# Layer 0 of a two-layer attention/FFN kernel: the band mask moves from a TensorE matmul into VectorE's row maximum

## The reference

```python
q, k, v = split(x @ w_in.T + b_in)                 # 8 heads of 8 channels, t = 256
scores = einsum('bqhd,bkhd->bhqk', q, k) / sqrt(d)
band = abs(idx[:, None] - idx[None, :]) <= 64      # local attention
scores = where(band, scores, neg)
attn = softmax(scores, axis=-1)
o = einsum('bhqk,bkhd->bqhd', attn, v) @ w_out.T + b_out
out = einsum('nit,io->not', relu(o^T) * encodings, w_ct) + b_ct
```

## Time and profile before

| | |
|---|---|
| median of 3 runs | 1429.04 us (1427.28 to 1431.03) |
| span of the profiled execution | 1429.4 us |
| TensorE, VectorE, ScalarE, GpSimd busy | 92%, 67%, 61%, 50% of the span |
| layer 0's attention, loads and weight preparation before it included | up to about 584 us |
| layer 0's FFN and the change of layers | about 584 to 700 us |
| layer 1's attention and FFN | from about 700 us |

### The profile page before, as it was taken

How to read it: one execution, slowest core, us unless ns; L and a number is a source line. 1 busy time by engine, 2 the same in 40 slices (tenths; PEclk the granted TensorE clock), 3 DMA queues, 4 the chain that set the end, 5 groups by cost and what they waited for, 6 DMA issues and landing times.

```text
span 1429.4 us, 37785 instructions
## 1 busy us (share of the span) xinstructions
PE 1315.2 (92%) x11332; PEld 910.0 (64%) x11332; DVE 955.8 (67%) x2156; ACT 874.6 (61%) x1909; POOL 716.5 (50%) x1292
## 2 busy tenths in 40 slices
PE   1999999999999998882799999999999989999998
PEld 1666777777777776571466666666666655766675
DVE  6438878787888787468888888888888872111110
ACT  1147676666666667563488888888888875122211
POOL 6336777777777776404555655656656511010000
PEclk9869999999999999995799999999999999999999
DMA  8314444444344443001434444444444410000000
GB/s 243 78 36 95 103 100 90 96 100 100 90 96 100 100 90 87 6 12 37 92 91 104 105 95 103 103 97 104 102 97 107 93 41 1 15 30 15 15 15 29
DMA packets 90797, 111.18 MB, mean 78 GB/s; under 512 B 15056, under 2 KB 82384, under 8 KB 83056
## 3 DMA queue, kind: packets, MB, share of 16 engines
q1 hardware_dynamic: 83184, 103.38, 31.9%
q10 hardware_dynamic: 7552, 7.02, 1.7%
HBM read 16.52 MB, written 4.19 MB: 14 GB/s over the span
## 4 chain that ended last, share of the span: by engine, by line
PE 62%; POOL 11%; issue 11%; DVE 8%; ACT 2%; ACTq 1%; DMA 1%; POOLq 1%; SPq 1%; DVEq 1%
PE bank L459 10%; PE bank L420 8%; PE bank L652 8%; PE bank L643 8%; PE bank L436 7%; PE bank L418 5%; PE bank L470 4%; DVE row_max L1031 3%; PE bank L501 3%; POOL rot L1216 2%; PE bank L614 2%; POOL Qp L1205 2%; PE bank L490 1%; POOL k_rest L1221 1%; POOL q_rest L1201 1%
## 5 line engine op out<-in xcount | busy, mean ns | idle before, releaser
L1031 DVE TENSOR_REDUCE row_max<-bank 128x2 f32<-128x384 f32 (+1 forms) x1024 | 599.6, 617 | 148.5 <-PE bank L420 146.8
L687 ACT ACTIVATE probs<-bank 128x384 f32<-128x384 f32 (+1 forms) x1024 | 534.4, 542 | 161.8 <-PE bank L436 155.0
L420 PE MATMUL bank<-Ks,Qs 96*128 96x192 bf16 (+1 forms) x2048 | 372.1, 264 | 13.5 <-DMA Ks<-Ks 8.4
L436 PE MATMUL bank<-Qs,Ks 128*128 128x192 bf16 (+1 forms) x2048 | 367.1, 261 | 13.6 <-ACT probs L687 12.5
L1234 POOL TENSOR_SCALAR_AFFINE_SELECT probs<-probs 128x256 f32<-128x256 f32 (+1 forms) x512 | 257.2, 526 | 175.1 <-ACT probs L687 156.3
L420 PEld LDWEIGHTS bank<-Ks,Qs 96*128 96x128 bf16 x2048 | 189.3, 99 | 122.8 <-issue 37.8
L459 PE MATMUL bank<-probs,V 128*32 128x192 f32 (+1 forms) x4096 | 249.0, 361 | 3.7 <-POOL probs L1234 2.4
L436 PEld LDWEIGHTS bank<-Qs,Ks 128*128 128x128 bf16 x2048 | 188.9, 98 | 40.1 <-ACT probs L687 23.9
L418 PE MATMUL bank<-band,ident 128*128 128x384 bf16 x512 | 169.2, 331 | 1.0 <-ACT out_bias L840 0.5
L459 PEld LDWEIGHTS bank<-probs,V 128*32 128x32 f32 x4096 | 107.4, 109 | 82.7 <-issue 41.8
L1171 DVE TENSOR_TENSOR X<-bank,X 128x256 f32 (+1 forms) x32 | 13.6, 425 | 184.6 <-PE bank L652 184.6
(11 more groups left out here) (128 smaller groups left out, 1776.9 us busy)
## 6 DMA issues: line engine op xcount, KB each, us to landing
Ks<-Ks SPq DMA_DIRECT2D x64, 576.0 KB
Qs<-Qs SPq DMA_DIRECT2D x128, 192.0 KB
Qs<-Qp SPq DMA_DIRECT2D x192, 64.0 KB
Ks<-Kp SPq DMA_DIRECT2D x192, 64.0 KB
side<-in_ctx SPq DMA_DIRECT2D x64, 128.0 KB, 2.0
X<-in_x ACTq DMA_DIRECT2D x4, 1024.0 KB, 10.4
out<-X SPq DMA_DIRECT2D x8, 512.0 KB, 2.9
Qs<-max_rows SPq DMA_DIRECT2D x128, 12.0 KB
```

The lines of the kernel that those rows point to most:

```text
L420: last = nc.tensor.matmul(dst[:, blk * win:(blk + 1) * win], Qs[0:SHIFT_ROW, pair[1], h, blk * P:(blk + 1) * P], Ks[0:SHIFT_ROW, pair[1], ...
L436: last = nc.tensor.matmul(dst[:, blk * win:(blk + 1) * win], Ks[:, pair[1], h, blk * P:(blk + 1) * P], Qs[:, pair[1], h, start(blk):start( ...
L687: nc.scalar.activation(probs[:, h % 8, 0:2 * win], exp_bank[h % 2][:, 0:2 * win], ACT.Exp, scale=SCALE).then_inc(s["exped"], 1)
L1031: nc.vector.tensor_reduce(row_max[:, pair[1], h, :], bank_of(pair, h)[:, 0:2 * win].rearrange("p (b k) -> p b k", b=2), AX.X, ALU.max).the ...
```

## The change

In layer 0 the band matmul is taken out of `score_head`; both score matmuls now stand alone (`start=True, stop=True`). In `maximum` the single `tensor_reduce` becomes two `tensor_tensor_reduce`, one per block of 192 columns: each adds `band16` to the scores, writes the sum back to the same PSUM columns and takes the maximum along the row into one column of `row_max`. The wait on `scored` goes through `wait_apart`. Layer 1 keeps its reduce.

```diff
@@ score_head
                 dst = bank_of(pair, h)
-                if l == 0:
-                    nc.tensor.matmul(dst[:, 0:2 * win], ident16[:, :], band16[:, :], start=True, stop=False)
                 for blk in range(2):
                     last = nc.tensor.matmul(dst[:, blk * win:(blk + 1) * win],
                                             Qs[0:SHIFT_ROW, pair[1], h, blk * P:(blk + 1) * P],
                                             Ks[0:SHIFT_ROW, pair[1], h, start(blk):start(blk) + win],
-                                            start=(l == 1), stop=(l == 1 or blk == 1))
+                                            start=True, stop=True)
@@ maximum
-                e.wait_ge(s["scored"], num(pair) * HPP + h + 1)
+                wait_apart(e, (s["scored"], num(pair) * HPP + h + 1))
+                if l == 0:
+                    for blk in range(2):
+                        part = slice(blk * win, (blk + 1) * win)
+                        last = nc.vector.tensor_tensor_reduce(out=bank_of(pair, h)[:, part], in0=bank_of(pair, h)[:, part],
+                                                              in1=band16[:, part], scale=1.0, scalar=OUTSIDE,
+                                                              op0=ALU.add, op1=ALU.max,
+                                                              accum_out=row_max[:, pair[1], h, blk:blk + 1])
+                    last.then_inc(s["maxed"], 1)
+                    return
```

## The result

The changed kernel takes 1473.8 us (median of 4 runs, 1472.3 to 1474.73) against 1429.88 before in the same series: ratio 1.031, 95% interval 1.029 to 1.033. The direction was right, the size was not, and the reason for the loss is another one: the prediction priced VectorE's new instructions too dearly and left out what their number does to VectorE's loop.

The account below looks back on a forecast made before the run. TensorE bounds layer 0's attention now; with the change VectorE would: 6.1 + 16 x 0.83 = 19.3 us per pair against 15.90, +3.4 us times 32 = +110 us on 1429.4, so 1540 us, range 1475 to 1690.

Parts of the forecast that it names:

- edits at nothing: Waits through `wait_apart` stay on the same instruction, layer 1's loop is unchanged: no cost, nothing changed from 584 us on.
- TensorE bounds now, VectorE has 2.42 us of slack: Layer 0's attention: TensorE busy 97% sets the 15.90 us pair; VectorE waits 2.42 us of it.
- The band matmul is worth 2.6 us per pair: TensorE, layer 0: sixteen band matmuls of 0.16 us leave the path; TensorE then needs 12.9 us per pair.
- The signs that the forecast named: Layer 0's attention: VectorE near 100% busy, hardly waiting for scores; TensorE about two thirds; period 19.3 us; clock 1.00.
- Fixed cost of an operation 0.13 us, read-out 0.09 us: VectorE's maxima, layer 0: two operations of 0.33 us plus two accumulator read-outs, 0.83 us per head against 0.46.
- zero, if it slips in beside the next operation: Lower bound for VectorE's accumulator read-out, taken at 0.09 us; the upper bound was 0.19.
- ScalarE's row: Profile row of ScalarE's similar accumulator read-out, 0.09 us from start to start, used to price VectorE's read-out.
- Everything else on VectorE stays at 6.1 us: VectorE's work per layer-0 pair besides the maxima (rests, splits, division, layernorm, residual): 6.1 us, unchanged.
- Rival 1: VectorE's new instructions run without overlap or at half rate: 1.2 to 1.24 us per head, about 1740 us; chance 0.12.
- Rival 2: TensorE, less busy in layer 0, drops to half clock for stretches: about 1600 to 1745 us; chance 0.07.
- Rival 3: Read-out free and small fixed cost of 0.07: 0.53 us per head, 1386 us; chance with its neighbourhood 0.06.
- decision point of 0.61 us per head: VectorE's cost per head in layer 0 that divides faster from slower: (15.90 - 6.1) / 16.

Follow-up runs that it names:

- the padded kernel: Kernel before, with four increments of an unused semaphore per head added to VectorE's layer-0 loop (body of 424 instructions, computing unchanged): 1465.1 us, ratio 1.025.

## Why the prediction was wrong, point by point

Two steps failed: the price of the new operation, where the read-out was put at 0.09 us and costs nothing, and the term "edits at nothing", where the longer loop body was put at zero and cost 38 us.

- *TensorE bounds now, VectorE has 2.42 us of slack.* Right, and the run with one increment per head confirms it: more instructions on VectorE that compute nothing (a body of 280) cost nothing.
- *The band matmul is worth 2.6 us per pair, and is not used, because VectorE becomes the bound.* Right in kind. With the loop written out VectorE is busy 97% and the pair takes 15.49 us, 0.4 us less than before. The signs that the forecast named are met only in part: in the changed kernel's loop TensorE is busy 83% and not two thirds, VectorE 84% and not near 100%, the clock is 0.94, and behind the gaps VectorE still waits for TensorE, which the forecast had named as a sign of being wrong.
- *Fixed cost of an operation 0.13 us, read-out 0.09 us.* This term was mis-sized, by the read-out. Measured: 0.316 us per operation, of which 0.20 are its columns, so 0.12 fixed, and the read-out nothing. The two read-outs of a head, 0.18 us, are 92 of the forecast's 110 us over 16 heads and 32 pairs. The bound "zero, if it slips in beside the next operation" was the true value, and ScalarE's row was the wrong one to take it from. A head costs 0.63 us and not 0.83. By the prediction's own sum 6.1 + 16 x 0.63 = 16.2 us per pair, measured 16.02: the sum was sound, and with the right price it gives some 4 to 10 us in all, not 110.
- *Everything else on VectorE stays at 6.1 us.* Nearly right for the looped form (16.02 - 16 x 0.63 = 5.9); the written-out one has 5.4.
- *Edits at nothing.* This is the step that failed altogether. The sum priced each new instruction by its time on the engine and none by the room that its code takes. The prediction saw four instructions where one stood and didn't count what that makes of the loop's body: 424 against 232. Nor do the waits "ride on the same instruction as before": each has one of its own, which is 48 of the 192. The branch back, free before, costs 3.1 us of VectorE and about 2.3 us of TensorE's clock, seven times, 38 us.
- "Layer 1's loop has the same instructions" was not so either: `wait_apart` gives it 48 such instructions more (179 to 227), below the length that hurts, and its pair took 15.2 us as before.
- *Rival 1*, every instruction paid dearly: wrong, an operation takes 0.316 us and the read-out is free. *Rival 2*, the clock: no steady loss, but the clock is 0.94 over the loop, mostly behind the gaps. *Rival 3*, faster: its decision point of 0.61 us per head was right for the looped form, and 0.63 lies just beyond it. Written out, 0.63 is already a gain of 7 us; with the sum written to SBUF as well (0.55) it is 29 us.
- The forecast of +110 for a measured +44 was thus two errors in opposite directions: the work over-priced by about 100 us, the branch left out with 38. That the direction came out right is in good part luck: by the forecast's own mechanism, rightly priced, the loss would have been 4 to 10 us.

The Trainium skill (Runtime: NRT & Kernel Launch, Instruction fetch mechanics) says that most engines hold 512 instructions of code, refilled in blocks of 256, and that a taken branch to a place outside the two blocks held stalls for a fetch. The runs agree in kind and put numbers to it that the page doesn't give: no stall at 232 and 280 instructions in the body, 2.5 to 3.5 us at 352 and 424, 4.0 at 838. By its 512 a body of 352 or 424 might have been thought safe; the measurement decides.

## What to carry to other kernels

Count what a change adds to the body of a hardware loop, on each engine, in instructions of the built program and not in operations: `tensor_tensor_reduce` with its accumulator output is two, and a helper that waits may add one. If a body grows past what a run has shown to be free (280 on VectorE here, while 352 was not), look in the trace for gaps of "issue" at the head of each round, and price them with what waits behind them, TensorE's clock included; writing out the loop of that one engine was all that was needed here.

When an instruction's full output is not wanted, its destination is a free choice: here bf16 in SBUF in place of fp32 in PSUM was worth 1.5%.

## What the runs showed of the hardware that was not expected

- VectorE's accumulator read-out has a row of 0.14 us (0.08 behind the form with its sum in SBUF) and takes no time of its own: the next operation starts at the same timestamp.
- `tensor_tensor_reduce` on 192 columns, an fp32 PSUM and a bf16 SBUF input, starts every 0.316 us with its output in PSUM as fp32 and every 0.275 us with it in SBUF as bf16.
- A branch back on VectorE's queue left it standing 3.1 us with 424 instructions in the body, 4.0 with 838, and not at all with 232 or 280. The profile shows no engine, semaphore or data DMA that it waited for, only an instruction packet in each gap.
- With TensorE's clock at half behind it, a gap of 3.0 to 3.5 us on VectorE cost 5.2 to 5.4 us of the whole.
- 128 semaphore increments in a row took VectorE 10.7 us, 0.08 us each. Four per head in the padded kernel left the pair at 15.9 us, between gaps, where VectorE had slack.
